# A gated attention block with a recurrence and a mixture of experts: denominators on TensorE, shorter candidate rounds, a held weight quarter, a last block in halves

## What is computed

```
x = x + tanh(g0) * wkv(time_decay, time_first, layernorm(x), ctx)
x = x + tanh(g1) * moe(layernorm(x), Wg, bg, W1, W2)

wkv, per channel, along the 256 steps of a sequence (k = layernorm(x), v = ctx):
    y_t = (sum of decayed exp(k_s) v_s, s < t, + exp(u + k_t) v_t)
        / (sum of decayed exp(k_s),     s < t, + exp(u + k_t))

moe: logits = x Wg + bg; the top 2 of 4 experts by softmax;
     each expert takes the 512 rows of highest weight p;
     out[row] += gelu(row W1[e]) W2[e] * p          (hidden width 2048)
```

## Time and profile before

| | us |
|---|---|
| median of 3 runs (lowest to highest) | 473.99 (473.29 to 474.87) |
| the profiled execution's own time | 473.74 |
| its span, first to last instruction | 471.8 |
| TensorE busy | 409.2 (87%) |
| VectorE busy | 291.8 (62%) |
| ScalarE busy | 313.4 (66%) |
| GpSimd busy | 109.7 (23%) |

### The profile page before, as it was taken

The page is one execution under the profiler, slowest core; times in us unless marked ns, Lnnn a source line. Parts: engine busy times, 40 slices in busy tenths (PEclk is TensorE's granted clock), DMA queues, the critical chain, the costliest instruction groups (busy, mean ns, idle before and its releaser), DMA issues.

```text
span 471.8 us, 6973 instructions
## 1 busy us (share of the span) xinstructions
PE 409.2 (87%) x1991; PEld 196.2 (42%) x1991; DVE 291.8 (62%) x596; ACT 313.4 (66%) x487; POOL 109.7 (23%) x126
## 2 busy tenths in 40 slices
PE   2686877812699999999999999999999999999991
PEld 1342443501464444444444444444444444444440
DVE  7999999988589986474575174457516435550000
ACT  6698888998569874766778790577879157760000
POOL 0787846601300002521000412100041210001111
PEclk9999999965599999999999999999999999999997
DMA  7985110399500629399000959500095510001211
GB/s 257 353 328 208 44 69 23 125 343 355 179 1 1 272 95 365 99 152 356 1 0 14 380 131 265 192 0 1 6 366 150 79 22 0 0 0 18 29 22 22
DMA packets 36182, 62.79 MB, mean 133 GB/s; under 512 B 14336, under 2 KB 14464, under 8 KB 34112
## 3 DMA queue, kind: packets, MB, share of 16 engines
q1 hardware_dynamic: 32064, 53.32, 32.6%
q0 software_dynamic: 3664, 8.65, 9.0%
q10 hardware_dynamic: 432, 0.54, 0.3%
HBM read 46.78 MB, written 12.58 MB: 126 GB/s over the span
## 4 chain that ended last, share of the span: by engine, by line
PE 74%; DVE 16%; issue 3%; ACT 2%; DMA 2%; POOL 2%; DVEq 0%; POOLq 0%
PE ps L813 35%; PE ps L798 26%; PE ps L778 7%; DVE arena L1278 6%; PE ps L741 2%; DVE arena L1297 2%; DVE arena L1308 2%; DMA arena<-xn_table,idx 1%; DVE arena L1533 1%; PE ps L617 1%; ACT early L874 1%; DMA small<-in_scalars 1%; POOL arena L1134 1%; PE ps L733 1%; DVE arena L1655 0%
## 5 line engine op out<-in xcount | busy, mean ns | idle before, releaser
L813 PE MATMUL ps<-arena 128*128 128x512 f16 x768 | 166.8, 379 | 0.0
L798 PE MATMUL ps<-arena,early 128*128 128x512 f16 x576 | 124.8, 379 | 0.0
L813 PEld LDWEIGHTS ps<-arena 128*128 128x128 f16 x768 | 74.6, 98 | 89.2
L798 PEld LDWEIGHTS ps<-arena,early 128*128 x576 | 56.4, 98 | 67.9
L1041 ACT ACTIVATE arena<-ps,up 128x512 f32<-128x512 f32 x64 | 43.8, 684 | 59.8 <-PE ps L798 41.2
L1707 DVE SCALAR_TENSOR_TENSOR arena<-arena,h_down 128x512 f32 x48 | 36.0, 751 | 58.8 <-ACT arena L1044 58.8
L1213 POOL DMA_INDIRECT result<-arena,idx x16 | 29.2, 1826 | 185.9 <-DVE arena L1735 122.7
L1044 ACT ACTIVATE arena<-arena,h_down 128x512 f32 x64 | 46.2, 721 | 8.7 <-ACT arena L1041 0.2
L1735 DVE TENSOR_SCALAR arena<-ps,yscale 128x512 f32<-128x512 f32 x16 | 12.0, 748 | 60.5 <-PE ps L813 49.2
L1686 DVE SCALAR_TENSOR_TENSOR early<-w_raw,down,early 128x2048 f16<-128x2048 f32 x16 | 37.0, 2345 | 18.8 <-ACT early L998 18.8
L1047 ACT ACTIVATE arena<-rows,down x64 | 45.2, 706 | 0.0
(11 more groups left out here) (224 smaller groups left out, 449.6 us busy)
## 6 DMA issues: line engine op xcount, KB each, us to landing
w_raw<-in_L_ffn_W SPq DMA_DIRECT2D x4, 4096.0 KB, 14.3
rows<-in_L_ffn_W SPq DMA_DIRECT2D x3, 4096.0 KB, 17.6
rows<-in_L_ffn_W SPq DMA_DIRECT2D x4, 1024.0 KB, 9.6
result<-rows SPq DMA_DIRECT2D x3, 1024.0 KB, 6.8
early<-in_ctx SPq DMA_DIRECT2D x2, 1024.0 KB, 6.9
rows<-in_x SPq DMA_DIRECT2D x2, 1024.0 KB, 12.0
xn_table<-arena SPq DMA_DIRECT2D x4, 512.0 KB, 5.1
xn_table<-arena SPq DMA_DIRECT2D x2, 1024.0 KB, 4.6
```

The source lines that it names most:

```text
L798: last = nc.tensor.matmul(ps[:, PH[q], :], w[:, k, at], t[:, k, :], start=n == 0, stop=n == 3 * CT - 1)
L813: last = nc.tensor.matmul(ps[:, PY[s % 2], :], h[:, t, s * P:(s + 1) * P], w[:, t, :], start=t == 0 and n == 0, stop=t == HT - 1 and n == 2)
```

## The change

The denominators of the long units are no longer computed by VectorE. The transposed exp(k) stays in its bank, and TensorE adds onto it a product of a diagonal matrix (c on the diagonal, made once by ScalarE from the identity) with the state; ScalarE's logarithm reads the sum from PSUM. `kv` is cut into `keys` and `products`, and TensorE's order of a long unit becomes add_first(u), products(u+2), xt(u), router(u-1), keys(u+2), residual_rows. In unit 2 xt comes ahead of the products.

```diff
@@ program, TensorE
+            def keys(u):
+                g, ct = u // CT, u % CT
                 if u >= 2:
-                    pe.wait_ge(s_den if GROUPS[g] > 1 else s_num, u - 1)
+                    pe.wait_ge(s_num, u - 1)
+                    if long(u - 2):
+                        pe.wait_ge(s_ln, u - 1)
                 for i, t in enumerate(tiles_of(g)):
                     if ct == 0:
                         pe.wait_ge(s_ek, t + 1)
-                    nc.tensor.transpose(pair(u, length(u) + i * P, length(u) + (i + 1) * P), ek[:, t % RING, ct * P:(ct + 1) * P], ident)
+                    last = nc.tensor.matmul(pair(u, length(u) + i * P, length(u) + (i + 1) * P), ek[:, t % RING, ct * P:(ct + 1) * P], ident,
+                                     start=i == 0 or not long(u), stop=True, is_transpose=True,
+                                            skip_group_check=True)
+                last.then_inc(s_keys, 1)
+
+            def add_first(u):
+                size = length(u)
+                if u == CT:
+                    pe.wait_ge(setup_a, 5 + CT)
+                pe.wait_ge(s_fix, u + 1)
+                nc.tensor.matmul(pair(u, size, 2 * size), first_diag[:, u % CT, :], state[:, u % 2, size:2 * size],
+                                 start=False, stop=True, skip_group_check=True).then_inc(s_denp, 1)
...
             for u in range(UNITS):
+                if long(u):
+                    add_first(u)
+                elif u + 2 < UNITS:
+                    keys(u + 2)
+                if u == LATE_M:
+                    xt(u)
                 if u + 2 < UNITS:
-                    kv(u + 2)
+                    products(u + 2)
                 if u == UNITS - 1:
                     residual_rows(TT - SPT - 1)
-                xt(u)
+                if u != LATE_M:
+                    xt(u)
                 if u > 0:
                     router(u - 1)
+                if long(u):
+                    keys(u + 2)
@@ ScalarE
+            act.wait_ge(s_id, 16)
+            for k in range(CT):
+                nc.scalar.activation(first_diag[:, k, :], ident, ACT.Copy, scale=chan[:, 3, k:k + 1]).then_inc(setup_a, 1)
...
-                act.wait_ge(s_den, u + 1)
+                if long(u):
+                    act.wait_ge(s_denp, u - shorts(u) + 1)
+                    there = pair(u, length(u), 2 * length(u))
+                else:
+                    act.wait_ge(s_den, shorts(u))
+                    there = den[:, u % 2, cols]
@@ VectorE, sums
-                if u >= 2:
-                    dve.wait_ge(s_ln, u - 1)
-                nc.vector.scalar_tensor_tensor(den[:, n, 0:size], ...
+                if not long(u):
+                    if u >= 2:
+                        dve.wait_ge(s_ln, u - 1)
+                    nc.vector.scalar_tensor_tensor(den[:, n, 0:size], ...
```

```diff
-                if r == 1:
-                    nc.vector.tensor_copy(base[:, 0:1], digit[:, 0:1]).then_inc(b_base, 1)
-                if r > 1:
-                    nc.vector.tensor_tensor(base[:, 0:1], base[:, 0:1], digit[:, 0:1], ALU.bitwise_or).then_inc(b_base, 1)
-                if 0 < r < ROUNDS0 - 1:
-                    dve.wait_ge(b_base, r)
-                    nc.vector.tensor_tensor(nxt[:, 0:1], base[:, 0:1], lane0(r + 1), ALU.bitwise_or).then_inc(b_next, 1)
                 dve.wait_ge(b_cnt, r + 1)
                 nc.vector.tensor_scalar(spot[:, :], cst[:, C_ONE0:C_ONE0 + LANES0], cnt[:, 0:1], None, ALU.mult).then_inc(b_spot, 1)
+                if 0 < r <= EXACT0:
+                    add_steps(r)
+                if r > EXACT0:
+                    nc.vector.tensor_tensor(base[:, 0:1], base[:, 0:1], digit[:, 0:1], ALU.bitwise_or).then_inc(b_base, 1)
+                if EXACT0 <= r < ROUNDS0 - 1:
+                    dve.wait_ge(b_base, r - EXACT0 + 1)
+                    nc.vector.tensor_tensor(nxt[:, 0:1], base[:, 0:1], lane0(r + 1), ALU.bitwise_or).then_inc(b_next, 1)
                 between(r)
...
+                if r < EXACT0:
+                    if r > 0:
+                        dve.wait_ge(b_sums, summed[r - 1])
+                    plus = cst[:, C_NEXT0:C_NEXT0 + 1] if r == 0 else sum_next[:, r - 1:r]
+                    nc.vector.tensor_scalar(cand[:, 0:1], took[:, r:r + 1], float(1 << shift0(r)), plus,
+                                            ALU.mult, ALU.add).then_inc(b_cand, 1)
```

`add_steps(r)` is three, two and one small VectorE operations in rounds 1, 2 and 3. Around the gather, SP holds w2's last quarter until the third gather has landed, and a second keep_warm follows the second count of the other experts; the last block of the last expert is done in two halves of 256 columns, each with its own eviction and indirect DMA:

```diff
             first_w2(2, (3,))
+            sp.wait_ge(c_tok[SPT], 16)
             first_w2(3, (4,))
@@
                 keep_warm(WARM)
                 others_round(1)
+                keep_warm(WARM)
                 pe.wait_ge(b_taken, 2)
@@
+            def last_halves():
+                for n in range(2):
+                    cols = slice(n * D // 2, (n + 1) * D // 2)
+                    pe.wait_ge(c_yout, START + (E - 1) * ST + (ST - 2))
+                    for t in range(HT):
+                        for i, (h, w) in enumerate(((h_hi, w2_hi), (h_hi, w2_lo), (h_lo, w2_hi))):
+                            last = nc.tensor.matmul(ps[:, LAST[n], 0:D // 2], h[:, t, (ST - 1) * P:ST * P], w[:, t, cols],
+                                                    start=t == 0 and i == 0, stop=t == HT - 1 and i == 2)
+                    last.then_inc(c_y, 1)
@@ GpSimd
-            scatter(E - 1, range(ST))
-            added(E - 1)
+            scatter(E - 1, range(ST - 1))
+            pool.wait_ge(c_yscs, START + 2 * E + 2)
+            for n in range(2):
+                cols = slice(n * D // 2, (n + 1) * D // 2)
+                pool.wait_ge(c_yout, START + (E - 1) * ST + ST + n)
+                hold(pool, "pool")
+                nc.gpsimd.indirect_dma_start(out_halves, bass.IndirectOffsetOnAxis(ap=idx_half[:, n:n + 1], axis=0),
+                                             y_c[:, (ST - 1) % 2, cols], None,
+                                             bounds_check=2 * N - 1, compute_op=ALU.add).then_inc(c_last[n], 16)
```

More of the change, by code:

```diff
@@ L65 @@
 C_LANE0 = C_ONE0 + LANES0
-C_ALL = C_LANE0 + ROUNDS0
+C_NEXT0 = C_LANE0 + ROUNDS0
+EXACT0 = 3
+C_ALL = C_NEXT0 + EXACT0
 S_TD, S_GATE, S_WG, S_BG = 0, 2 * CT, 2 * CT + 2, 2 * CT + 2 + CT * E
@@ L76, in shift0, with ones0 @@
     return DIGIT0 * (ROUNDS0 - 1 - r)
+def ones0(r):
+    return sum(1 << shift0(i) for i in range(r + 1))
 def tiles_of(g):
@@ L132, in constant_table @@
     lane = np.arange(P, dtype=np.int32)[:, None] % LANES0
-    t[:, C_LANE0:] = np.concatenate([lane << shift0(r) for r in range(ROUNDS0)], 1).astype(np.int32).view(np.float32)
+    for r in range(EXACT0):
+        t[:, C_NEXT0 + r] = (lane[:, 0] << shift0(r + 1)) - ones0(r)
+    t[:, C_LANE0:C_NEXT0] = np.concatenate([lane << shift0(r) for r in range(ROUNDS0)], 1).astype(np.int32).view(np.float32)
     return t
@@ L141, in program @@
     out_rows = out.rearrange("b s d -> (b s) d")
+    out_halves = out.rearrange("b s (a d) -> (b s a) d", a=2)
     out_v = out_rows.rearrange("(t p) d -> p t d", p=P)
@@ L204, in program @@
         decay = part(arena, at, (CT, 2 * UN))
-        den = part(arena, at, (2, UN))
+        den = part(arena, at, (2, SEQ))
+        first_diag = part(arena, at, (CT, P))
         num = part(arena, at, (2, UN))
@@ L275, in program @@
         cnt = sb("cnt", [P, 2])
+        took = sb("took", [P, ROUNDS0])
+        sum_next = sb("sum_next", [P, EXACT0])
+        sum_base = sb("sum_base", [P, EXACT0])
         spot = sb("spot", [P, LANES0], F16)
@@ L478, in length, with long, shorts @@
             return GROUPS[u // CT] * SEQ
+        def long(u):
+            return GROUPS[u // CT] > 1
+        def shorts(u):
+            return sum(not long(i) for i in range(u + 1))
         def starts(ap, u):
@@ L837, in _ @@
             up_product(E - 1)
-            for s in range(ST):
+            for s in range(ST - 1):
                 down_block(E - 1, s)
+            last_halves()
         @block.scalar
@@ L1107, in scales1 @@
                     hold(pool, "pool")
-                    nc.gpsimd.tensor_scalar(var1[:, some], sq1[:, there], 1.0 / D, EPS, ALU.mult, ALU.add).then_inc(s_var1, 1)
+                    nc.gpsimd.tensor_scalar(var1[:, some], sq1[:, there], 1.0 / D, EPS, ALU.mult, ALU.add).then_inc(s_nb, 1)
                 else:
@@ L1508, in between, with add_steps @@
                     power_of(1, 0)
-                    nc.vector.tensor_scalar(less16[:, :], cst[:, C_TRI:C_TRI + P], -1.0, None, ALU.add).then_inc(s_mats, 1)
                 elif r == 4:
                     bounded_power(1, 0)
-                    nc.vector.tensor_copy(group16[:, :], cst[:, C_GRP:C_GRP + P]).then_inc(s_mats, 1)
                 elif r == 5:
                     scales_of(1, 0)
-                    nc.vector.tensor_copy(tri16[:, :], cst[:, C_TRI:C_TRI + P]).then_inc(s_mats, 1)
+            made = [EXACT0, 2 * EXACT0 - 1]
+            summed = [1, EXACT0 + 1]
+            def add_steps(r):
+                size = float(1 << shift0(r - 1))
+                if r > 1:
```

(10 more changed lines are left out.)

120 lines of the change are left out of this document (74 added, 46 removed).

## The result

The changed kernel runs in 466.46 us (median of 4 runs, 465.99 to 467.92), against 474.07 for the kernel before beside it (4 runs). The ratio is 0.9848, 95% interval 0.9823 to 0.9873: 7.6 us faster, 1.5%. The prediction said 465.5, 462.5 to 470.0. The profiled execution took 466.88, its span 464.9, so 6.9 of span stand to be found.

What follows compares the result with a forecast made beforehand. VectorE was taken to bound the recurrence stage, with ScalarE close behind and the likely next bound. Gains of 4.5 + 1.1 + 2.2 + 0.7 = 8.5 us from 473.74, with the median 0.25 higher, gave 465.5, range 462.5 to 470.0.

Steps and rivals of the forecast that it cites:

- Part 1: Long units: moving denominators from VectorE to TensorE gains 4.5 us, bounds 0 and 7.9.
- ScalarE's floor: Long units: ScalarE becomes the likely bound; of its 5.9 us of waits 1.4 remain, so 4.5 is gained.
- the cover of 0.6: Long units: quotient ends 3.9 us after its start point, residual due at 4.5; ScalarE later than 0.6 stalls VectorE.
- TensorE as the bound: Rival, long units: product costs 1.4 or more, or its wait stalls x's transposes; 4.5 lost, 470.0 us; chance 0.14.
- VectorE's whole 7.9: Rival, long units: ScalarE doesn't bound and VectorE's full 7.9 us comes through; 462.1 us; chance 0.07.
- The slower rival: Long units: TensorE's clock falls, 3.1 us per unit; four such units give 477.9 us; chance 0.04.
- Part 2: Candidate rounds: one operation for digit and candidate, base operations moved into a wait; gains 1.1 us, bounds 0.6 and 1.3.
- Part 3: Gather stretch: holding back a w2 quarter and a second keep_warm gain 2.2 us, bounds 0 and 2.6.
- The clock's 1.0: After the gather: the first group's 16 products at full clock take 1.8 us instead of 2.81, 1.0 less.
- give-back of "0 to 1": After the gather: the held w2 quarter lands late, so 0 to 1 us of the gain comes back.
- Part 4: Last block in halves: smaller last eviction and transfer, less slower products; gains 0.7 us, bounds 0 and 1.2.
- The 472.5 for "no change": Rival: stalls eat the long units' 0.66, gate and last block give 0.7 together; 472.5 us; chance 0.05.

Runs made afterwards that it cites:

- e1: Kernel after with the long units' denominators put back on VectorE and the diagonal matrices removed; 470.40 us, ratio 0.9926.
- e6: Kernel after with GpSimd multiplying a unit's row tiles ahead of the second norm's scales; 465.49 us, ratio 0.9838.
- e11: Kernel after with the edits of e6 and e7, and the second norm's first scales moved behind the next unit's quotient; 464.31 us, ratio 0.9815.
- e12: e11 plus unit 11's scales behind that unit's quotient and one of w1's half rows summed behind the logits; 463.60 us, ratio 0.9798.
- e7: Kernel after with TensorE transposing x ahead of the products in every long unit; 466.0 us.
- e8: Kernel after with TensorE transposing x twice in every long unit, as added work; 467.88 us.
- e2: Kernel after with the candidate rounds of the kernel before (digit, then bitwise or; base between count and spot); 467.67 us.
- e5: Kernel after without the second group of four products that keep TensorE busy, the gate on w2's last quarter kept; 467.46 us.
- e3: Kernel after with the last block whole again instead of in halves; 467.78 us, ratio 0.9881.
- e4: Kernel after without the gate on w2's last quarter, the second busy group kept; 467.67 us.
- e10: Kernel after with neither the gate on w2's last quarter nor the second busy group; 468.65 us.

## Why the prediction was right

The forecast case held: faster, with the gain in the four places named. Point by point:

- **Part 1, 4.5 predicted: 3.1 by the traces of before and after, 3.4 by e1.** The failing step is "ScalarE's floor is its present time less its waits ... 1.4 remain". 4.1 of its waits remain. The 1.6 for a scale among them is the 1.4 foreseen; the 2.5 for TensorE's sum (L620) had been put at nothing. That sum is now at the end of TensorE's in-order queue, which stands 3.8 for GpSimd's row tiles. The text had named what stands behind add_first, but not what stands ahead of it: the transposes that wait for GpSimd. Nor was ScalarE the floor: 5.9 - 4.1 would be a gain of 1.8, and 3.1 came. What the time follows is VectorE's residual, which waits 4.0 for the quotient.
- **Where the 1.4 went.** From the fifth to the seventeenth scan, the twelve long periods, it is 49.61 instead of 54.14: 4.53 less, beside a forecast of 4.5 that was reached by other waits, so that the agreement is luck. What is missing is lost behind them, where the forecast has "in the four short units at the end nothing is removed" and says of added waits nothing. A short unit's work stands before the last long unit's residual, so it is due 78.57 - 1.41 - 73.52 = 3.6 after its unit's numerators start (at 73.52), and not 4.5 after them. Against the quotient's 3.9 the cover of 0.6 is gone there, even before TensorE comes late. The period from the seventeenth to the eighteenth scan grew from 2.90 to 4.40, and it is still 3.4 in e6 and 3.8 in e11 and e12.
- **What the order on GpSimd gives.** With e6's, e7's and e11's edits the first count comes at 83.58 from the first scan, 2.1 to 2.3 earlier than in the kernel after; with e12's two edits and one half row gone from the stage at 82.93, 5.8 earlier than before's 88.78.
- **Its rivals.** TensorE as the bound: refuted by e8 (5.3 more work, 1.4 later), though the margin is small. VectorE's whole 7.9: needs no waits at all; 1.9 are left in e12. The product's cost, taken as 0.95 with 1.76 as upper end: from the row at 69.78 to the next at 70.66 it is 0.88. (The Trainium skill, FP8 and Floating Point Precision, "TensorE Precision Notes", counts four passes for a true float32 product; an estimate from that, 4 x 512 columns at 2.4 GHz, is 0.85. The trace agrees.)
- **The slower rival, the clock falling in long units**: in the kernel after it didn't happen. In one of twelve traces with the product on TensorE (the kernel after and e2 to e12) it did, in one unit (e5), for 1.5 and not the 3.1 priced. It had its place right (behind a wait of TensorE), and had been put off with "the change makes those stretches shorter"; the waits for row tiles are stretches it did not remove.
- **Part 2, 1.1 predicted: 0.95, and 1.1 by e2.** Right in size. The split was off: the one operation saves 0.13 (0.25 against 0.38), not 0.19, since it takes 0.21 itself where the bitwise or took 0.16. "They go into the wait for the column sums" held: VectorE waits 0.25 for these sums in round 0 and not at all in the rounds that have the small operations.
- **Part 3, 2.2 predicted: 1.57 in the profiled execution, 2.0 against the mean of ten traces.** The clock's 1.0 came as 0.90 (2.81 to 1.91); e5 puts the second busy group at 0.9. The 16 products started 5.33 - 4.06 = 1.27 earlier, of the 1.5 for the tiles. The give-back of "0 to 1" was 0.6 in this trace and 0.2 in the mean of the ten. A tile landed 3.5 after its gather's issue in e5, as the sum had it; in the kernel after the second busy group stood before it until 4.4, beyond the "3.5 to 4" given as a sign. So each term came out near its size, and each a little to the worse side in this trace. What the text did not have is that the two edits stand in each other's way: the busy group covers part of the earlier landing, and without the busy group half of that landing is lost to the low clock. And 0.5 of the stretch is explained by neither.
- **Part 4, 0.7 predicted: 1.27 (1.39 in the tail less 0.12).** The eviction's 0.3 was 0.27 and the products' loss 0.12. The mis-sized term is the bytes, taken with 0.5 to 1.0 and entered near the low end: 1.01 from the issue to the end (e3). By the slope that the Trainium skill gives (DMA: Bandwidth & Descriptors, "Anatomy of one DMA") it would have been 0.3, an estimate; the trace doesn't agree, an accumulating indirect store of half the bytes ended 1.0 earlier.
- **Slips in the working.** From the gather's issue to the tile's use it is 124.23 - 118.75 = 5.5, not 5.4. The 472.5 for "no change" does not follow from what is named for it: 473.99 - 0.7 is 473.3. Neither bears on the forecast.

The errors of 1.4, 0.15 and 0.6 on one side and 0.57 on the other leave 8.5 - 6.9 = 1.6, of which run-to-run spread takes some: the medians stand 7.6 apart.

## What to carry to other kernels

An operation moved to an engine with slack joins that engine's queue. What the row of its own cost doesn't show is what stands ahead of it there, and for whom that waits: here transposes that waited for a third engine, whose order (scales before rows) had cost little as long as no path led through it. After such a move, read the waits of the receiving engine first and reorder its feeders; that was worth 2.2 on top of the change's 7.6, and 2.9 with the two edits of e12. Look also at the first unit behind the stretch that gets shorter: its work is shorter and covers less, and 1.5 of the 4.9 gained by the long units' end was lost again there. For a last store, halving it saved the bytes' time too (1.0), not the eviction's alone (0.3).

## What the runs showed of the hardware

- TensorE's granted clock fell to 0.50 (1.2 GHz) inside the long units in two of the thirteen traces of the kernel after and its versions: in e1 from 44 us on, after an idle of 2.02 at 41 to 43, and in e5 from 40 on, after the waits of 0.69 and 0.90 at 37 to 39. The kernel before kept 1.00 until 80 us. Eleven traces kept 1.00 throughout, e3 and e4 with the same instructions and the same waits as e5 among them, so one trace doesn't tell whether a program has this cost. It cost nothing where VectorE was the bound and 1.5 where TensorE's sum was on the path.
- An operation on VectorE of one element per row that writes int32 from float32 took 0.15 with two constants (digit) and 0.21 with a constant and an operand per row (candidate). With the same operands and a float32 result it took 0.20 to 0.21 (the small sums), so the operand and not the type goes with the 0.06.
- The gather's first tile was there 3.5 after its issue with the last w2 quarter held back (e5), and 5.2 without (e4, e10), one trace for the first and two for the second. Each is the moment at which a waiting TensorE starts on it.
